# Router logits in the experts' stage: weights held in the array, x streaming past, and a turn behind the up products

## The reference

```python
xf = _layernorm(x)                               # 10000 x 512
logits = xf @ Wr + br                            # Wr: 512 x 8
probs = jax.nn.softmax(logits, axis=-1)
vals, idx = jax.lax.top_k(probs, 2)
cw = (jax.nn.one_hot(idx, 8) * vals[..., None]).sum(axis=1)
for e in range(8):                               # a scan in the reference
    h = relu(xf @ W1[e] + b1[e])                 # 512 x 64
    out += cw[:, e, None] * (h @ W2[e] + b2[e])  # 64 x 512
x = x + out
```

## Time and profile before

| | |
|---|---|
| median of three runs | 2564.85 us |
| the profiled execution | 2563.35 us |
| its span, first to last instruction | 2561.7 us |
| mean granted TensorE clock | 0.999 of full speed |
| busy share of the span: PE, DVE, ACT, POOL | 98%, 74%, 58%, 41% |
| first router matmul of the experts' stage | 1926.6 us from the start |
| last group of router matmuls begins | 2540.87 us |

### The profile page before, as it was taken

One profiled execution on the slowest core, in us unless ns is written; L12 is line 12 of the kernel. 1 busy time (PEld: TensorE's weight loads), 2 busy tenths in 40 slices (PEclk: granted clock), 3 DMA queues, 4 the chain that ended last, 5 costly groups with the idle time before them and its releaser, 6 DMA issues.

```text
span 2561.7 us, 40284 instructions
## 1 busy us (share of the span) xinstructions
PE 2512.7 (98%) x9906; PEld 1632.2 (64%) x9906; DVE 1899.7 (74%) x5059; ACT 1485.4 (58%) x3471; POOL 1043.6 (41%) x1293
## 2 busy tenths in 40 slices
PE   8999999999999999999999999999999999999999
PEld 4444445555488875555468885555547888888887
DVE  5555555556599976555589996557748999999997
ACT  2222245555288865555458885555525666666665
POOL 3222245555244435555333333555533333333332
PEclk9999999999999999999999999999999999999999
DMA  4444468888355548888735556998842334533331
GB/s 148 132 133 133 129 190 262 271 265 272 100 165 165 164 159 272 267 271 264 229 105 165 163 167 230 320 323 259 268 147 89 100 100 141 168 100 96 100 102 63
DMA packets 208171, 460.91 MB, mean 180 GB/s; under 512 B 34895, under 2 KB 35207, under 8 KB 208004
## 3 DMA queue, kind: packets, MB, share of 16 engines
q0 software_dynamic: 64928, 207.55, 28.6%
q1 hardware_dynamic: 73812, 125.17, 14.1%
q10 hardware_dynamic: 69264, 126.12, 13.4%
HBM read 245.32 MB, written 213.93 MB: 179 GB/s over the span
## 4 chain that ended last, share of the span: by engine, by line
PE 93%; DVE 3%; issue 1%; DMA 1%; ACT 1%; ACTq 0%; another core or an unknown queue 0%; POOL 0%; DVEq 0%; SPq 0%; POOLq 0%
PE psY L678 11%; PE psY L792 9%; PE psM L792 9%; PE psH L792 8%; PE psY L692 6%; PE psY L700 6%; PE psY L709 6%; PE psT L658 5%; PE psS L804 4%; PE psS L805 4%; PE psY L879 3%; PE psH L913 3%; PE psH L926 3%; PE psY L882 3%; PE psY L891 3%; PE psH L917 3%
## 5 line engine op out<-in xcount | busy, mean ns | idle before, releaser
L564 POOL DMA_INDIRECT rows<-y_rows,lists x471 | 491.3, 1043 | 471.9 <-PE psS L805 318.4
L1336 DVE TENSOR_TENSOR lows<-rows,highs 128x512 fp32r<-128x512 f32 x471 | 325.9, 692 | 356.0 <-ACT highs L960 322.2
L960 ACT ACTIVATE outs<-psS 128x512 f32<-128x512 f32 x471 | 279.5, 593 | 282.5 <-PE psS L805 249.2
L960 ACT ACTIVATE highs<-rows 128x512 fp32r<-128x512 f32 x471 | 294.7, 626 | 147.4 <-ACT outs L960 95.7
L804 PE MATMUL psS<-highs,sel 128*128 128x512 f32 x471 | 346.5, 736 | 13.0 <-ACT outs L960 8.4
L571 POOL DMA_INDIRECT rows<-sum_rows,nodeI x158 | 210.3, 1331 | 312.9 <-DVE rows L1344 297.2
L678 PE MATMUL psY<-wy,res 128*128 128x512 f32 x632 | 286.5, 596 | 0.0
L960 ACT ACTIVATE outs<-psY 128x512 f32<-128x512 f32 x237 | 141.6, 598 | 231.2 <-PE psY L678 221.5
L792 PE MATMUL psM<-wz,res 128*128 128x512 f32 x544 | 255.4, 592 | 0.0
L792 PE MATMUL psY<-wz,res 128*128 128x512 f32 x536 | 251.7, 592 | 0.0
L792 PE MATMUL psH<-wz,res 128*128 128x512 f32 x528 | 247.9, 592 | 0.0
(11 more groups left out here) (204 smaller groups left out, 4918.3 us busy)
## 6 DMA issues: line engine op xcount, KB each, us to landing
sum_rows<-outs ACTq DMA_DIRECT2D x471, 256.0 KB
y_rows<-outs SPq DMA_DIRECT2D x237, 256.0 KB, 2.0
rows<-in_x POOLq DMA_DIRECT2D x78, 256.0 KB, 3.2
outs<-in_x SPq DMA_DIRECT2D x78, 256.0 KB
out_rows<-res SPq DMA_DIRECT2D x78, 256.0 KB, 2.0
rows<-y_rows,lists POOLq DMA_INDIRECT x471
z_rows<-res SPq DMA_DIRECT2D x13, 512.0 KB
res<-z_rows SPq DMA_DIRECT2D x13, 512.0 KB, 4.0
```

The costliest lines, as they stand in the source:

```text
L564: pool.indirect_dma_start(out=rows[:, t % RING, :], out_offset=None, in_=y_d, in_offset=bass.IndirectOffsetOnAxis(ap=col(srcT, t), axis=0) ...
L960: act.activation(o, i_, ACT.Copy).then_inc(signal, 1)
L1336: dve.tensor_tensor(lows[:, t % RING, :], rows[:, t % RING, :], highs[:, g, :].bitcast(F32), ALU.subtract)\
```

## The change

The router's product is turned round. `wg2` (128 x 16) is held as weights and x streams past it: one matmul for each of the four blocks of 128 features, with 256 columns moving, 128 of the high part of x and 128 of the low part (`x_both` joins the two buffers so that one access pattern spans both). The result lies in `psM[0:16, 0:256]`, with the 16 columns of `wg2` on partitions. ACT copies it to `logitT` in SBUF, negated (`take_logits`, a new step of ACT between `h_top(k - 2)` and `norm(k + 1)`). PE turns it back by two 128x128 transposes (`router_turn`, a new step between `up_parts(k)` and `x_turn(k + 1)`) into `psM[:, 256:512]`. DVE adds the four partial logits of each expert by one reduce over a strided view and subtracts the bias; this pair now stands behind line 1499 rather than ahead of it.

```diff
-        xhs = nc.alloc_sbuf_tensor_at("xhs", [P, 2, D], F32R, offset=wy_at)
-        xls = nc.alloc_sbuf_tensor_at("xls", [P, 2, D], F32R, offset=wy_at + 8 * D)
+        x_both = nc.alloc_sbuf_tensor_at("x_both", [P, 2, 2, D], F32R, offset=wy_at)
+        logitT = nc.alloc_sbuf_tensor_at("logitT", [P, 2 * P], F32, offset=wz_at + 12 * D)
+        xhs = x_both[:, 0]
+        xls = x_both[:, 1]
...
             def router(k):
-                s, n = k % 2, k // 2
+                s = k % 2
                 pe.wait_ge(xh_set, (LAYERS - 1) * NT + k + 1)
                 pe.wait_ge(xl_set, (LAYERS - 1) * NT + k + 1)
+                pe.wait_ge(logit_set, k)
+                for q in range(C):
+                    mm = pe.matmul(psM[0:2 * X, 0:2 * P], wg2[:, q, :], x_both[:, :, s, q * P:(q + 1) * P],
+                                   start=(q == 0), stop=(q == C - 1))
+                mm.then_inc(router_ps, 1)
+
+            def router_turn(k):
+                s = k % 2
+                pe.wait_ge(logit_set, k + 1)
                 if k > 0:
                     pe.wait_ge(lg_sb[1 - s], (k - 1) // 2 + 1)
-                for q in range(C):
-                    pe.matmul(psM[:, 0:2 * X], xhs[:, s, q * P:(q + 1) * P], wg2[:, q, :], start=(q == 0), stop=False)
-                for q in range(C):
-                    mm = pe.matmul(psM[:, 0:2 * X], xls[:, s, q * P:(q + 1) * P], wg2[:, q, :], start=False,
-                                   stop=(q == C - 1))
+                for j in range(2):
+                    mm = pe.transpose(psM[:, (2 + j) * P:(3 + j) * P], logitT[:, j * P:(j + 1) * P], ident[:, :])
                 mm.then_inc(lg_ps[s], 1)
...
                 router(k)
                 up_parts(k)
+                router_turn(k)
                 if k + 1 < NT:
                     x_turn(k + 1)
...
+            def take_logits(k):
+                s, n = k % 2, k // 2
+                act.wait_ge(router_ps, k + 1)
+                if k > 0:
+                    act.wait_ge(lg_ps[1 - s], (k - 1) // 2 + 1)
+                act.activation(logitT[0:2 * X, :], psM[0:2 * X, 0:2 * P], ACT.Copy, scale=-1.0).then_inc(logit_set, 1)
...
                     h_top(k - 2)
+                take_logits(k)
                 if k + 1 < NT:
                     norm(k + 1)
...
-                if own:
-                    dve.wait_ge(lg_ps[s], n + 1)
-                    k_lg = step(dve.scalar_tensor_tensor(gate(LG), psM[:, 0:X], -1.0, bgs[:, :],
-                                                         ALU.mult, ALU.subtract))
-                    after(k_lg)
-                    k_lg = step(dve.tensor_tensor(gate(LG), gate(LG), psM[:, X:2 * X], ALU.subtract))
                 if ahead:
...
                     k_a = step(dve.scalar_tensor_tensor(a, a, degree, own_x, ALU.mult, ALU.add))
                 if own:
+                    dve.wait_ge(lg_ps[s], n + 1)
+                    parts = psM[:, 2 * P:4 * P].rearrange("p (h r) -> p h r", h=2)[:, :, 0:2 * X]
+                    k_lg = step(dve.tensor_reduce(gate(LG), parts.rearrange("p h (g e) -> p e h g", g=2), AX.XY, ALU.add))
+                    after(k_lg)
+                    k_lg = step(dve.tensor_tensor(gate(LG), gate(LG), bgs[:, :], ALU.subtract))
                     after(k_lg)
                     dve.tensor_reduce(stat(LOWEST), gate(LG), AX.X, ALU.min).then_inc(lg_sb[s], 1)
```

More of the change, by code:

```diff
@@ L289, in build @@
         pad_set = sem("pad_set")
+        router_ps = sem("router_ps")
+        logit_set = sem("logit_set")
         block = ctx.enter_context(nc.Block())
```

## The result

Seven runs of the changed kernel gave a median of 2573.54 us (2572.27 to 2575.09), seven of the kernel before 2564.85 us. The ratio is 1.0037, with a 95% interval of 1.0026 to 1.0047. The forecast was 2574.7 us, between 2567 and 2582. The profiled execution took 2573.3 us, with a span of 2571.7 us, 10.0 us more than the span before.

The account below looks back on a forecast made before the run. DVE was taken to set the period of the experts' stage: 75 tiles x 0.09 = +6.8 us, start +3.3, end -0.3, together +9.8 us, forecasting 2574.7 us, range 2567 to 2582.

Parts of the forecast that it names:

- Who sets the period: Experts' stage, steady state: DVE, never idle, sets the 7.91 us period; PE has some 0.15 us to spare each tile.
- the first step: What bounds the kernel now: DVE releases PE, so what the change takes from PE is worth nothing in steady state.
- The first rival: PE sets the period and DVE only follows closely: each of 77 tiles gains 0.15 us, 2555 us; chance 0.09.
- The third rival: New router matmuls cost 0.23 us each, so PE bounds: period about 8.08, 2582 us, deciding from 0.21 us a matmul; chance 0.11.
- DVE's term: DVE's small instructions from 1472 to 1507: 1.14 us grows by 0.09 a tile, +6.8 us over 75 tiles (4.5 to 9.8).
- Start: First tiles, where DVE waits for the late turn: tile 0 +1.2, tile 1 +2.6, tile 2 -0.5, together +3.3 us.
- its lower case: First tiles with the clock at full speed in tile 1, the turn there 1.6 us sooner: +1.7 us.
- tile 0's term: Tile 0: the turn ends at 1929.4, so 1507 comes at 1929.9 in place of 1928.72: +1.2 us.
- The total: Whole kernel: steady tiles +6.8, start +3.3, end -0.3, together +9.8 us, giving 2574.7 us; chance 0.69.
- Router, turn, copy, end: PE's router matmuls 0.46 us and two transposes 0.22, ACT's copy about 0.37, last two tiles -0.3 us in all.
- The exponential: ACT's exponential, called 0.1 us later each tile, is hidden, as the reduce's logits have 0.6 us to spare.
- The second rival: The dependent wait costs nothing, or pipelining pays the reduce's turn back: tiles neutral, only the start remains, 2568 us; chance 0.11.

Follow-up runs that it names:

- e1: Kernel before with only DVE's part of the change (reduce, subtraction, minimum behind line 1499), router, PE and ACT as before: period 8.03 us, ratio 1.0034.
- e2: Kernel before with one added DVE wait and no more work: line 1499 waits for 1494, which it does not need: period 8.04 us, ratio 1.0045.
- e9: Kernel before, old router kept; second logit instruction and minimum each moved behind a long DVE line, ACT's widening ahead of the exponential: period 7.89 us, ratio 1.0004.
- e3: Kernel before with a ninth router matmul on PE in each tile (the first one done twice): period 7.96 us, ratio 1.0023.
- e4: Changed kernel with the bias given to ACT's copy in place of DVE's subtraction: period 7.82 us, ratio 0.9991.
- e7: Changed kernel with the turn of the logits ahead of the up products in tiles 0 and 1 only: period 8.03 us, 2573.23 us (one run).
- e8: Changed kernel with ACT's widening of the up product put ahead of the exponential: period 8.03 us, ratio 1.0036.
- e5: e4 with DVE's minimum moved behind the next 512-element line, so nothing waits for a small instruction: period 7.95 us, ratio 1.0023 to the kernel before.
- e10: Changed kernel with bias on ACT, widening first, and two small PE matmuls turning and adding the logits in place of transposes and DVE's reduce: 8.15 us period, ratio 1.0087.

## Why the prediction held, and where it was off

**Who sets the period: right, by less than I thought.** DVE sets it (e1, e2), and PE's saving of 0.36 - 0.22 = 0.14 us came to nothing, as the first step said. But PE's spare time was 0.02 to 0.06 us (e9, e3), not 0.15, as I had taken the idle time of the weight load for idle time of the array. The first rival was wrong about who bounds the kernel, but the two engines were within 1% of each other. The third rival's sum has the same fault: with 7.85 to 7.89 us in place of 7.91 - 0.15, I estimate that it would have decided from 0.18 to 0.19 us a matmul, not from 0.21.

**DVE's term: right in kind, 0.02 us too small.** 0.115 us a tile against my 0.09, 8.6 us against 6.8. The count by distances gave 1.24 us and the trace has 1.25 to 1.26: the reduce and the subtraction each cost 0.21. I had rounded down.

**Start: wrong by half, and its lower case right by luck.** I took 3.3 us, of which 1.6 were for a low clock in tile 1, and named 1.7 for a clock at full speed. It was 1.75 us. The clock stayed at full speed in tile 1 and fell in tile 2, to 0.54 between 1939.5 and 1941.5 us, after PE had waited 1.83 us for the widening. (In e4 it did fall in tile 1, and that tile took 8.52 us, not 7.29.) Only tile 0's term was right, 1.22 us against 1.2. In tile 1 I had 1.0 us at full clock from the late turn. 1526 does start 0.92 us later after `xls`, but the tile grew by 0.53 us, as DVE had before waited there for the exponential and now has the turn's wait in its place; e7 shows that the 0.53 is not the turn's. And the 0.5 us that I took off for `h_high` in tile 2 did not come: that wait grew from 0.48 to 0.63 us. It comes behind `xls` of tile 2, so it is counted in the 8.6 us of the steady part.

**The total: right by luck.** 1.8 us too little in the steady part and 1.6 too much in the start cancel. Each was off by a fifth to a half, and the sum is right to 0.2 us only by that.

**Router, turn, copy, end.** 0.47, 0.22 and 0.37 us and -0.3 us, against 0.46, 0.22, 0.37 and -0.3. (The low bound of the end should have been -0.4, not -0.6: 2 x (0.42 + 0.22 - 0.83).) The third rival (0.23 us a matmul) is out: 256 columns cost 0.12 us, half of 512.

**The exponential was not hidden.** I said that its being 0.1 us later was covered. PE has stood still for 0.27 us a tile since then, ahead of the cross products. It cost nothing, since PE was not the bound (e8), but the step as written was wrong, and e5 shows what it costs once DVE is shorter.

**The second rival** (dependent waits free, the rule of the Trainium skill, "VectorE: DVE Perf Modes", section "The DRAIN you can't avoid", which was measured on copies) fell with e2: 0.12 us for one wait ahead of an instruction that needs nothing of it, and a stage 10 us longer (622.4 against 612.1 us).

## What to carry to other kernels

Where two engines are both nearly full, ask which shows no wait, count the start-to-start distances of that one, and then add a little work or a wait to each in turn: the view alone misjudged PE's spare time here, and hid a wait of DVE in e3. A change that relieves the other engine and adds a dependent small instruction to this one was a loss here. A small instruction on DVE cost 0.08 us with an independent one behind it and 0.2 with a dependent one, so weave it between long ones, but follow who waits for its result round the loop first. What was lost on one engine may still be the condition for a gain: with the subtraction on ACT, the woven minimum and the widening first, the same router gives 0.9949 of the time before.

## What the runs showed of the hardware

The idle time ahead of a weight load said little about the array: with 0.19 us of it a tile, the matmuls had 0.02 to 0.06 us to spare (e9, e3). A plain float32 matmul of 16x128 weights with 8 moving columns ran as two matmuls, 0.13 us each (0.53 / 4, in e10), where a 128x128 transpose cost 0.11. And a wait of 0.06 us showed as no idle time in DVE's timeline: e3's first addition starts 0.67 us, not 0.61, behind the instruction ahead of it, and has no releaser beside it.
